# The experts' up product with the weights as stationary operand, and the first weights loaded tile by tile

## What is computed

```python
B, S, D, F, E = (8, 256, 512, 256, 8)      # here 4096 rows of 512, F = 256 hidden, 8 experts
xf = x.reshape(-1, D)
logits = xf @ router_w
gate_vals, idx = jax.lax.top_k(logits, K)  # K = 2
gates = jax.nn.softmax(gate_vals, axis=-1)
for e in range(E):
    h = jax.nn.relu(xf @ w1[e] + b1[e]) @ w2[e] + b2[e]
    y = _layernorm(xf + h, gamma[e], beta[e])
    w = jnp.sum(jnp.where(idx == e, gates, 0.0), axis=-1)
    out = out + w[:, None] * y
```

## Time and profile before

| what | value |
|---|---|
| median of 3 executions | 3353.06 us (3352.49 to 3356.41) |
| the profiled execution, its span | 3357.4 us |
| start of `experts` up to the first up product | 2823 us to 2923.9 us |
| the 72 tiles, first up product to the last `outer` | 2923.9 us to about 3262 us |
| the last sums | about 3262 us to the end |
| busy in 2950 to 3250 us: TensorE, VectorE, GpSimd, ScalarE | 280.9, 268.8, 244.7, 155.2 of 300 us |
| DMA in 2950 to 3250 us | 113 GB/s, 0.36 of the 16 DMA engines |

### The profile page before, as it was taken

How to read it: one execution, slowest core, us unless ns; L and a number is a source line. 1 busy time by engine, 2 the same in 40 slices (tenths; PEclk the granted TensorE clock), 3 DMA queues, 4 the chain that set the end, 5 groups by cost and what they waited for, 6 DMA issues and landing times. The chain is left out here.

```text
span 3357.4 us, 51640 instructions
## 1 busy us (share of the span) xinstructions
PE 2711.2 (81%) x11877; PEld 1690.1 (50%) x11877; DVE 2583.3 (77%) x5129; ACT 1697.2 (51%) x5677; POOL 2132.7 (64%) x2164
## 2 busy tenths in 40 slices
PE   6987888862888888886998888887999998699970
PEld 5544444431333333333555555556888885366640
DVE  8766666642999999998999999996665663489874
ACT  5222222211666665666988888884434432355540
POOL 2777777776777777776777777772222220188876
PEclk8888888875999999998999999997999998899995
DMA  4544444452777777776777777774111112633338
GB/s 165 171 146 145 149 148 146 145 188 85 211 210 208 209 207 210 210 210 183 213 213 214 214 214 214 214 215 131 51 51 51 51 55 77 232 114 114 114 109 286
DMA packets 212182, 545.15 MB, mean 162 GB/s; under 512 B 49457, under 2 KB 58545, under 8 KB 207026
## 3 DMA queue, kind: packets, MB, share of 16 engines
q0 software_dynamic: 121984, 345.93, 36.8%
q1 hardware_dynamic: 89906, 195.92, 16.9%
HBM read 466.45 MB, written 75.25 MB: 161 GB/s over the span
## 5 line engine op out<-in xcount | busy, mean ns | idle before, releaser
L1225 PE MATMUL at_pair<-product,v_hot 128*128 128x260 f32 x2304 | 624.0, 401 | 85.2 <-DVE product L976 28.2
L1176 PE MATMUL at_pair<-wide,hot_t 128*128 x1152 | 579.0, 619 | 122.9 <-ACT hot_t L1028 107.5
L811 POOL DMA_INDIRECT fetched<-t_k,at_index x576 | 551.7, 958 | 183.2 <-issue 122.5
L821 POOL DMA_INDIRECT fetched<-t_v,at_index x576 | 546.9, 950 | 185.7 <-issue 110.9
L357 POOL DMA_INDIRECT records<-staged,address x544 | 539.1, 991 | 188.2 <-issue 161.9
L1225 PEld LDWEIGHTS at_pair<-product,v_hot 128*128 128x128 f32 x2304 | 394.1, 190 | 311.0 <-issue 143.5
L648 PE MATMUL qkv_prod<-wide 128*128 128x512 f32 x768 | 398.9, 683 | 94.3 <-ACT wide L397 87.4
L968 DVE TENSOR_TENSOR wide<-at_pair,wide 128x520 f32 x576 | 400.5, 695 | 34.1 <-issue 18.8
L895 DVE TENSOR_TENSOR product<-at_pair,fetched 128x512 f32<-128x512 f32 x576 | 392.9, 684 | 39.0 <-DMA fetched<-t_k,at_index 28.6
L1176 PEld LDWEIGHTS at_pair<-wide,hot_t 128*128 128x128 f32 x1152 | 187.5, 189 | 380.9 <-issue 377.7
L1114 ACT ACTIVATE product<-fetched,act_weight 128x65 f32<-128x65 f32 x1152 | 335.1, 338 | 82.9 <-DMA fetched<-t_v,at_index 75.3
(11 more groups left out here) (304 smaller groups left out, 4534.9 us busy)
## 6 DMA issues: line engine op xcount, KB each, us to landing
row_bc<-in_src SPq DMA_DIRECT2D x34, 1024.0 KB, 5.2
by_slot<-m_y SPq DMA_DIRECT2D x72, 256.0 KB, 2.0
low_bc<-low_row SPq DMA_DIRECT2D x34, 512.0 KB, 6.3
wide<-in_x SPq DMA_DIRECT2D x64, 256.0 KB, 3.6
fetched<-t_k,at_index POOLq DMA_INDIRECT x576, 3.7
fetched<-t_v,at_index POOLq DMA_INDIRECT x576, 3.7
records<-staged,address POOLq DMA_INDIRECT x544, 2.3
t_v<-wide SPq DMA_DIRECT2D x32, 260.0 KB
```

The source lines that it names most:

```text
L811: eng.indirect_dma_start(fetched[:, n % SLOTS, 0:C], None, k, bass.IndirectOffsetOnAxis(index[:, t:t + 1], 0)).then_inc(s_row[n % SLOTS], 16)
L821: eng.indirect_dma_start(fetched[:, n % SLOTS, :], None, v, bass.IndirectOffsetOnAxis(index[:, t:t + 1], 0)).then_inc(s_row[n % SLOTS], 16)
L1176: nc.tensor.matmul(q_edge[u % 4], hot_t[:, g % 2, u % BATCH * P:(u % BATCH + 1) * P], q_sb[:, bass.ds(at, 1), :].rearrange("p a c -> p (a ...
L1225: last = nc.tensor.matmul(pair[u % 3][:, n, 0:HALF], hot[:, u % 4, :], product[:, u % 4, n * HALF:(n + 1) * HALF], start=True, stop=True)
```

## The change

Two things are changed, both in `experts`.

**The up product is made the other way round.** Now the expert's `w1`, in pieces of 128x128, is the stationary operand, and the turned rows `zT` move. The result has the hidden units on the partitions and the rows in the columns, which is what `down` needs. So `hidden` (ScalarE's copy), `turn_hidden` (TensorE's two transposes), `h_sb` and `h_turned` are gone, and `hidden_columns` reads `up_ps`. In place of four products with 256 columns there are eight with 128 (two pieces f of the hidden units by four pieces kc of the width).

**`w1` is no longer kept in SBUF for all experts.** `w1_sb` has `AHEAD` = 4 buffers in place of 8. SyncE loads the 512 KB of one tile's expert for every tile, in rows of 1 KB. Three loads are issued ahead; then the body of tile u issues the load of tile u + 3, waits for `e_done` of u, and issues the store of u. The load waits for `e_up` of tile u - 1, whose buffer it takes, and TensorE's `up` waits for the load (`e_w1`). The load of 4096 KB at the start is gone, and `s_w` is waited for at 80.

```diff
-        w1_sb, w2_sb = sb("w1", [P, E, KC, F]), sb("w2", [P, E, FC, C])
+        w1_sb, w2_sb = sb("w1", [P, AHEAD, KC, F]), sb("w2", [P, E, FC, C])
...
-            eng.dma_start(w1_sb[:, :, :, :], w1.rearrange("e (k p) f -> p e k f", p=P)).then_inc(s_w, 16)
...
+            by_expert = w1.rearrange("e (k p) f -> p e k f", p=P)
+
+            def load_w1(i, u):
+                e = expert(eng, i, u)
+                e_up.wait(eng, i, u - AHEAD)
+                eng.dma_start(w1_sb[:, u % AHEAD, :, :], by_expert[:, e, :, :].rearrange("p a k f -> p (a k) f")
+                              ).then_inc(e_w1.sem(u), 16)
+
+            eng.wait_ge(s_ready, 1)
+            for u in range(AHEAD - 1):
+                load_w1(0, u)
+
             def store(i, more):
                 for u in range(TURN):
+                    ahead, at = divmod(u + AHEAD - 1, TURN)
+                    if not ahead or more:
+                        load_w1(i + ahead, at)
                     e_done.wait(eng, i, u)
                     eng.dma_start(tile_rows(by_slot, i, TURN, u), y[:, u % 4, :]).then_inc(e_put.sem(u), 16)
...
-            def up(i, u, e):
+            def up(i, u):
+                e_w1.wait(eng, i, u)
                 e_zT.wait(eng, i, u)
-                for kc in range(KC):
-                    last = nc.tensor.matmul(up_ps[u % 2][:, :], zT[:, u % 2, kc * P:(kc + 1) * P], flat(w1_sb[:, e, kc, :]),
-                                            start=(kc == 0), stop=(kc == KC - 1))
+                e_hT.wait(eng, i, u - 2)
+                for f in range(FC):
+                    for kc in range(KC):
+                        last = nc.tensor.matmul(up_ps[u % 2][:, f * P:(f + 1) * P], w1_sb[:, u % AHEAD, kc, f * P:(f + 1) * P],
+                                                zT[:, u % 2, kc * P:(kc + 1) * P], start=(kc == 0), stop=(kc == KC - 1))
                 last.then_inc(e_up.sem(u), 1)
-
-            def turn_hidden(i, u):
-                e_h.wait(eng, i, u)
-                for f in range(FC):
-                    last = nc.tensor.transpose(h_turned[u % 2][:, f * P:(f + 1) * P], h_sb[:, u % 2, f * P:(f + 1) * P],
-                                               ident[:, :])
-                last.then_inc(e_hturn.sem(u), 1)
```

More of the change, by code:

```diff
@@ L1705, in experts @@
     assert SLOTS % TURN == 0
+    AHEAD = 4
     HALF = 4
@@ L1771, in experts @@
         turned = [ps(f"turned{b}", [P, C]) for b in range(2)]
-        up_ps = [ps(f"up{b}", [P, F]) for b in range(2)]
-        h_turned = [ps(f"h_turned{b}", [P, F]) for b in range(2)]
+        up_ps = [ps(f"up{b}", [P, FC * P]) for b in range(2)]
         down_ps = [ps(f"down{b}", [P, C]) for b in range(2)]
@@ L1792, in experts @@
         s_top = sem("top")
-        names = ("e_turn", "e_zT", "e_up", "e_h", "e_hturn", "e_hT", "e_down", "e_res", "e_y", "e_var", "e_root",
+        names = ("e_turn", "e_zT", "e_up", "e_hT", "e_down", "e_res", "e_y", "e_var", "e_root",
                  "e_x3", "e_base", "e_gain", "e_done", "e_index")
-        (e_turn, e_zT, e_up, e_h, e_hturn, e_hT, e_down, e_res, e_y, e_var, e_root, e_x3, e_base, e_gain, e_done) = (
+        (e_turn, e_zT, e_up, e_hT, e_down, e_res, e_y, e_var, e_root, e_x3, e_base, e_gain, e_done) = (
             Ring([sem(n)], TURN) for n in names[:-1])
         e_index = Ring([sem("e_index")], 2)
+        e_w1 = Ring([sem(f"e_w1{b}") for b in range(AHEAD)], TURN, 16)
         e_put = Ring([sem(f"e_put{b}") for b in range(4)], TURN, 16)
@@ L1823, in _ @@
         def _(eng):
-            for r in (e_put, c_out):
+            for r in (e_put, c_out, e_w1):
                 r.start(eng)
@@ L1936, in _ @@
         def _(eng):
-            for r in (r_zT, r_hot_p, e_zT, e_h, e_hT, e_x3):
+            for r in (r_zT, r_hot_p, e_zT, e_hT, e_x3):
                 r.start(eng)
@@ L1961, in columns @@
                 nc.scalar.copy(zT[:, u % 2, :], turned[u % 2][:, :]).then_inc(e_zT.sem(u), 1)
[L1963 to L1966, removed]
             def hidden_columns(i, u):
                 e = expert(eng, i, u)
-                e_hturn.wait(eng, i, u)
+                e_up.wait(eng, i, u)
                 e_down.wait(eng, i, u - 2)
                 for f in range(FC):
-                    last = nc.scalar.activation(hT[:, u % 2, f, :], h_turned[u % 2][:, f * P:(f + 1) * P], ACT.Relu,
+                    last = nc.scalar.activation(hT[:, u % 2, f, :], up_ps[u % 2][:, f * P:(f + 1) * P], ACT.Relu,
                                                 bias=flat(b1_sb[:, e, f:f + 1]))
@@ L1984, in _ @@
             outer(0, 0)
-            hidden(0, 0)
             hidden_columns(0, 0)
@@ L2144, in _ @@
         def _(eng):
-            for r in (r_turn, r_route, r_route_turned, r_listed, e_turn, e_up, e_hturn, e_down):
+            for r in (r_turn, r_route, r_route_turned, r_listed, e_turn, e_up, e_down):
                 r.start(eng)
@@ L2232, in _ @@
             turn_rows(0, 1)
-            up(0, 0, expert(eng, 0, 0))
-            turn_hidden(0, 0)
+            up(0, 0)
             def body(i, more):
@@ L2243, in body @@
                         e = expert(eng, i, u + 1)
-                        up(i, u + 1, e)
+                        up(i, u + 1)
                     down(i, u, this)
-                    if u < TURN - 1 or more:
-                        turn_hidden(i, u + 1)
             by_turn(TURNS, body)
```

10 lines of the change are left out of this document (4 added, 6 removed).

## The result

The changed kernel takes **3475.22 us** (median; 3472.24 to 3481.01), the kernel before 3354.36 us on the same chip: a ratio of 1.036, with a 95% interval of 1.0347 to 1.0373. It is 121 us slower. The forecast was 3428 us, 75 us slower, with 3388 to 3490 as its range. The sign and the loop that the forecast named hold; the size is short by 47 us.

A forecast was written before the change was run, and what follows sets the result against it. TensorE, VectorE and their hand-overs were taken to share the bound at 4.66 us a tile; a w1 round trip of 5.77 us adds 1.11 us on 68 tiles, about 75 us with 1 us gained, giving 3428 us, range 3388 to 3490.

The forecast's parts named there:

- the loop that the forecast named: Tile stage: `e_done`, SyncE's w1 load, `up`, `down`, sum and variance, `outer`; 11.5 us over two tiles, 5.77 a tile.
- The deciding term: w1 load per tile on SyncE: 5.0 us wanted where 1.9 to 3.1 are there, so TensorE waits; +75 us.
- The pieces of the round: Over two tiles: issue 1.2, landing 3.8, hand-over 0.05, `up` 1.85, down to sum 1.92, to `outer`'s end 2.41, stretch 0.3 us.
- the clock as a rival: TensorE in the tile stage: idle gaps of 3.1 us lower the granted clock; 3475 to 3545 us, chance 0.2.
- The forecast's price: Low clock on TensorE's `up` and `down`: 3.4 us a round, 58 us in half of 34 rounds, 116 in all.
- The loop's own bounds: Two-tile round trip over SyncE at 5.2 to 6.5 us a tile: +37 to +125 us, so 3389 to 3478.
- The turned product: Up product on TensorE: ScalarE's copy and its wait go, TensorE's time stays; 18 to 36 us over 72 tiles.
- hidden in the wait: Tile stage: TensorE's 4.2 us a tile lies below the round trip's 5.77, so the turned product's saving does not show.
- The landing by the Trainium skill's figure: w1 load: 2.0 us plus bytes over 436 GB/s, 3.2 us for 512 KB; round trip 10.9 us, tile 5.5.
- the weights are there in time: w1 loads land before `up` needs them, so TensorE's 4.2 or VectorE's 4.4 us binds; 3320 to 3334 us, chance 0.05.
- Most signs: Tile stage profile: w1 wait 1 to 2 us a tile, tiles every 5.3 to 6.3, TensorE 0.75 busy, landing 3.3 to 4.7.
- The one named as a contradiction: Tile stage: the forecast is wrong if the granted clock leaves 1.00; no size was given to this sign.

The follow-up runs named there:

- the run with filler: Changed kernel plus three more float32 products of 256 columns on TensorE before each up product, into spare PSUM that nobody reads: 3436.06 us, ratio 1.0244.
- the loads alone: Kernel before the change with w1 loaded tile by tile into four buffers as in the change, but the old up product, copy and transposes: 3470.41 us, ratio 1.0333.

## Why the prediction was right in kind and short in size

- **The deciding term.** The load stands behind the store of its tile, and the loop over it spans two tiles. Confirmed by the chain in the trace, by the gain when the load leaves the loop (1.036 to 0.998 in two ways) and by the gain when only a part of the loop is made shorter.
- **The pieces of the round.** From `outer`'s end to the issue: 1.1 us (3052.98 to 3054.07) for 1.2. Landing: 3.9 in the median for 3.8, and 4.1 to 4.3 in the rounds shown. `outer`: 0.85 us where nothing stretched it, and a mean of 1.23 in the stage, for 0.75 + 0.3. The sum at full clock: 11.6 for 11.5. Each term is within 0.1 us or a few tenths.
- **The step that failed: the clock as a rival, and not as a term.** The forecast's own working had TensorE stand for 3.1 us in each round, and held against the rival that the clock stayed at 1.00 after gaps of 0.86 us and that only light products had run ahead of a gap that lowered it. But 0.86 is far from 3.1, and the one row at about that length, 2.86 us, was after all the right one: the clock fell after a wait of 2.57 us behind dense products. Instead of 20% for a case of its own, the term belonged in the sum, with the rounds in which it falls as the unknown. The term's size was off too. The forecast's price was 3.4 us a round, up and down product both slow throughout, in half or all of 34 rounds. Measured were 25 of 34 rounds at 1.75 us, about half of the price, since the clock was low for only a part of the two products: 44 us by that count, 39 by the run with filler. With the latter the sum is 75 + 39 = 114, and 121 was measured; 5 of the 7 us left are the base, since the 4.66 us a tile of before are the pace of a part of the stage and all 72 tiles have 4.58 (68 x 0.08). The rival as written said 3475 to 3545, but its own sum gives 3428 + 58 = 3486 as the lower end. So 3475 was no hit of the rival's. The loop's own bounds, 3389 to 3478, held it as well, but by luck: their upper end was made of a landing of 4.7 us and more stretch of `outer`, and neither came. The Trainium skill, TensorE: Matmul & The Clock Gate, section "Why this matters for your kernels", warned of idle gaps between bursts; the granted clock of 0.91 here, and 1.00 with filler at 39 us less, agree.
- **The turned product.** It was costed at 18 to 36 us where nothing else comes later, and gave 28; the number is right in part by luck. The forecast took all of it from the round trip over ScalarE and let TensorE's own time stand. It was said to be hidden in the wait, and was: both halves together are no faster than the loads alone. TensorE's own time was put at 4.1 to 4.2 us and is 3.95: sixteen short records cost no more than eight wide ones, so the two transposes' 0.22 us stay as a gain. From 4.20 to 3.95 us is 18 of the 28 us over 72 tiles. The rest came with less waiting, which the forecast had, and a shorter `outer`, which it had not.
- **The landing by the Trainium skill's figure.** The Trainium skill, DMA: Bandwidth & Descriptors, section "Anatomy of one DMA", has its figure for GpSimd's kind of DMA; by the forecast's estimate from it 512 KB land in 3.2 us. For SyncE's loads 3.9 in the median and 3.7 at best were measured. The rows of this case were nearer.
- **What the forecast did not have.** It held traffic in time for free ("the weights are there in time", 3320 to 3334; the 4.4 us of VectorE in that rival stand in no row, its busy time of 0.90 of 4.66 is 4.2). Kernels in which they are in time take 3350 us, 16 to 30 more, and the long meetings of `outer` with GpSimd are the likely reason. This did not touch the forecast, since in the slow rhythm of the changed kernel they hardly occur: one `outer` of 48 in the changed kernel lasts over 2.5 us.
- **What would have shown it.** Most signs came: the wait for w1 ahead of `up` (1.6 us a tile in the mean), 6.29 us a tile at the upper end of 5.3 to 6.3, TensorE busy 0.74, 3.9 us to land. The one named as a contradiction, a clock below 1.00 in the stage, came too, and it makes up some 40 of the 47 us. Two signs came only in part: `up` took 1.9 to 2.1 us at the full clock alone, and the DMA moved 165 GB/s for 182, as the rhythm was slower.

The fastest kernels found that compute the whole of the reference are those with the loads on ScalarE's queue, at 0.9976 and, with long rows, 0.9968 of before; the one with eight buffers, at 0.9982, is not clearly behind. They hold the changed kernel's four buffers of w1 and gain 0.2 to 0.3%. The larger gain, 47 us, was seen only with most of beta left out; whether the two additions can be kept apart in a kernel that has both was not tried.

## What to carry to other kernels

A load that is issued behind a store inherits the store's wait. Write out the loop from the consumer back to the issue with the landing, and count how many tiles it spans: where the sum is more than that many tiles' time, the load is the bound, though the DMA share be low (0.52 here). And where a loop leaves TensorE idle for some microseconds in each round, the lower clock's price belongs in the sum: here 1.75 us in 25 of 34 rounds.

## What the runs showed of the hardware

- A load of 512 KB landed in 3.9 us in the median at a DMA share of 0.52, in 3.6 at 0.59 with filler, in 4.2 to 5.0 at 0.72 to 0.77; one of 256 KB took 2.8 at 0.48.
- Rows of 4 KB for rows of 1 KB shortened the landing of 512 KB by 0.2 to 0.3 us, and the kernel's time by no more than its uncertainty.
- Sixteen float32 records of 128 columns with a new stationary block each took 1.79 us up to the next product, 0.112 us each. The eight of 256 columns had taken 1.83 us.
- A VectorE operation with both inputs in SBUF, 0.75 us alone, took up to 3.76 us when it began up to 0.7 us before two additions on GpSimd that follow one another; with one of them cut short it took at most 1.84 us.
- Of 34 waits of 2 to 4.7 us between dense products (1.2 GHz behind the one of 2.57 us shown), 25 had slow products behind them, at 1.75 us each in the mean; 9 of 3.0 to 3.6 us had none.
- Adding three needless products a tile made the kernel 39 us faster; TensorE's granted clock was 1.00 (2.4 GHz) with them and 0.91 without.
